# A transformer layer over 1,024 sequences: the order of ScalarE's transfers, and of the turn, cast and split of x, is changed

## The reference, cut to what matters

```
q = x @ wq + bq;  k = x @ wk + bk;  v = x @ wv + bv      # 8 heads of 16
out  = softmax(q k^T / 4) v                               # per head, over 128 tokens
x1   = layernorm(x + out @ wo + bo, ln1_g, ln1_b)
ff   = relu(x1 @ w1 + b1) @ w2 + b2                        # 512 hidden features
y    = layernorm(x1 + ff, ln2_g, ln2_b)
```

## Time and profile before

| | |
|---|---|
| median of three runs | 4492.08 us |
| the profiled execution | 4491.22 us, its span 4489.4 us |
| TensorE busy, matmul and weight load | 4162.2 us (93%), 3558.9 us (79%) |
| VectorE busy | 3687.2 us (82%) |
| ScalarE busy | 3503.9 us (78%) |
| GpSimd busy | 3694.0 us (82%) |
| granted TensorE clock, mean | 0.993 |

### The profile page before, as it was taken

How to read it: one execution, slowest core, us unless ns; L and a number is a source line. 1 busy time by engine, 2 the same in 40 slices (tenths; PEclk the granted TensorE clock), 3 DMA queues, 4 the chain that set the end, 5 groups by cost and what they waited for, 6 DMA issues and landing times.

```text
span 4489.4 us, 150530 instructions
## 1 busy us (share of the span) xinstructions
PE 4162.2 (93%) x49930; PEld 3558.9 (79%) x49930; DVE 3687.2 (82%) x9740; ACT 3503.9 (78%) x5890; POOL 3694.0 (82%) x3864
## 2 busy tenths in 40 slices
PE   5999999999999999999999999999999999999997
PEld 4888787878888888888778788878888887888886
DVE  5888888888888888888888888888888888888885
ACT  3787777778777878777778777878777877778786
POOL 4888888888888888888878888888888888888887
PEclk7999999999999999999999999999999999999999
DMA  7777777777777777777777777777777777777773
GB/s 141 169 168 176 166 176 168 174 167 178 172 170 173 171 173 168 175 169 175 169 170 168 171 169 173 169 173 169 175 167 176 168 176 168 174 169 175 172 171 85
DMA packets 1970442, 755.81 MB, mean 168 GB/s; under 512 B 1181312, under 2 KB 1969536, under 8 KB 1969664
## 3 DMA queue, kind: packets, MB, share of 16 engines
q1 hardware_dynamic: 1662480, 605.71, 60.9%
q10 hardware_dynamic: 307184, 140.40, 11.3%
HBM read 202.51 MB, written 134.22 MB: 75 GB/s over the span
## 4 chain that ended last, share of the span: by engine, by line
PE 23%; POOL 23%; issue 19%; ACT 12%; ACTq 11%; DVE 11%; POOLq 0%; SPq 0%; DMA 0%; DVEq 0%
POOL rs L314 9%; ACTq L459 7%; POOL xT_parts L330 7%; ACT parts L385 6%; PE bankA L740 6%; PE bankA L663 5%; DVE st L557 5%; PE bankC L663 4%; DVE z_sb L581 4%; POOL o_sb L286 3%; ACTq L472 3%; PE sT_ps L714 3%; PE s_ps L700 3%; ACT h_sb L392 2%; ACT v_ones L467 2%
## 5 line engine op out<-in xcount | busy, mean ns | idle before, releaser
L412 ACT ACTIVATE prob_sb<-sT_ps 128x1024 f32<-128x1024 f32 x1024 | 1044.2, 1020 | 238.0 <-PE sT_ps L714 127.5
L540 DVE TENSOR_REDUCE max_sb<-s_ps 128x8 f32<-128x1024 f32 x1024 | 1220.7, 1192 | 8.3 <-PE s_ps L700 7.3
L700 PEld LDWEIGHTS s_ps<-stack 96*128 96x128 bf16 x8192 | 464.5, 98 | 261.8 <-issue 236.6
L700 PE MATMUL s_ps<-stack 96*128 96x128 bf16 x8192 | 640.3, 221 | 17.9 <-DVE max_sb L540 10.3
L714 PE MATMUL sT_ps<-stack 99*128 99x128 bf16 x8192 | 628.6, 219 | 2.3 <-ACT prob_sb L412 2.2
L278 POOL TENSOR_TENSOR parts<-rest_sb,parts 128x512 bf16<-128x512 f32 x512 | 583.7, 1159 | 40.5 <-ACT parts L385 32.9
L392 ACT ACTIVATE h_sb<-bankC,b_col 128x512 f32<-128x512 f32 x512 | 352.0, 688 | 319.1 <-issue 315.5
L434 ACT ACTIVATE n_sb<-z_sb,shift,rs 128x128 f32<-128x128 f32 x1024 | 422.3, 483 | 196.9 <-POOL shift L316 196.9
L727 PE MATMUL oT_ps<-prob_sb,v_ones 128*32 128x128 f32 x16384 | 554.3, 276 | 4.3 <-ACT prob_sb L412 3.3
L686 PE MATMUL bankB<-w_sb,h_sb 128*128 128x128 f32 x4096 | 526.7, 282 | 6.1 <-ACT h_sb L392 5.8
L727 PEld LDWEIGHTS oT_ps<-prob_sb,v_ones 128*32 128x32 f32 x16384 | 416.6, 109 | 127.8 <-issue 90.7
(11 more groups left out here) (75 smaller groups left out, 8919.6 us busy)
## 6 DMA issues: line engine op xcount, KB each, us to landing
stack<-parts SPq DMA_DIRECT2D x3072, 128.0 KB, 3.5
x_blocks<-in_x SPq DMA_DIRECT2D x1024, 64.0 KB, 2.3
n_mem<-n_sb SPq DMA_DIRECT2D x256, 256.0 KB, 2.5
n_blocks<-n_mem SPq DMA_DIRECT2D x1024, 64.0 KB, 2.2
out<-out_sb ACTq DMA_DIRECT2D x256, 256.0 KB, 4.3
x_sb<-in_x ACTq DMA_DIRECT2D x255, 256.0 KB, 3.6
stack<-max_parts ACTq DMA_DIRECT2D x768, 8.0 KB, 2.3
h_sb<-in_L_conv_w SPq DMA_DIRECT2D x1, 256.0 KB, 3.2
```

The costliest lines, as they stand in the source:

```text
L412: act.activation(prob_sb[:, s % 2], sT_ps[:], ACT.Exp, scale=float(D) ** -0.5).then_inc(exp_done, 1)
L540: dve.reduce_max(max_sb[:, (r - lag) % 2, :, s], s_ps[:].rearrange("p (h k) -> p h k", h=H), AX.X).then_inc(max_done, 1)
L700: ins = pe.matmul(s_ps[:, h * P:(h + 1) * P], stack[0:PROD, (r - lag) % 4, 0, h, tok], stack[0:PROD, (r - lag) % 4, 1, h, tok], start=True ...
```

## The change

Four things are written in another order; nothing is added and nothing removed.

1. The three transfers of maxima no longer follow one another: the first stands behind relu 0, the second behind relu 1, the third behind the copy of v.
2. The load of x for the residual moves from the end of step r - 1 to step r, behind the cast of xT.
3. VectorE turns x right after row maximum 0, ahead of z; it was after row maximum 1.
4. ScalarE casts xT right after exponential 0, ahead of relu 2 and 3; it was after the four `n_sb`. GpSimd splits xT ahead of the deviations; it was after the first `normalise`.

```diff
@@ GpSimd
+                if live(t, r, 0):
+                    pool.wait_ge(xT_hi, upto(t, r, 0, plus=1))
+                    if (v := upto(t, r, 0)) is not None:
+                        pool.wait_ge(k_done, v)
+                    pool.tensor_tensor(xT_parts[:, REST], xT_sb[:], xT_parts[:, HI].bitcast(F32),
+                                       ALU.subtract).then_inc(xT_lo, 1)
                 if live(t, r, 5) or live(t, r, 8):
...
                 if live(t, r, 4):
                     normalise(t, r, 0)
-                if live(t, r, 0):
-                    pool.wait_ge(xT_hi, upto(t, r, 0, plus=1))
...
@@ ScalarE
+            def max_row(t, r, part):
+                act.dma_start(stack[PROD + part:PROD + part + 1, (r - 2) % 4, 0],
+                              max_parts[:, part]).then_inc(max_rows_loaded, DMA)
...
                 exponentials(t, r, 0)
+                if live(t, r, 0):
+                    act.wait_ge(x_turned, upto(t, r, 0, plus=1))
+                    if (v := upto(t, r, 0)) is not None:
+                        act.wait_ge(k_done, v)
+                    act.activation(xT_parts[:, HI], xT_sb[:], ACT.Copy).then_inc(xT_hi, 1)
+                if live(t, r, 0) and (r > 0 or not isinstance(t, int)):
+                    if (v := upto(t, r, 1)) is not None:
+                        act.wait_ge(xb_done, v)
+                    act.dma_start(x_sb[:, r % 2], x_g[t + r]).then_inc(x_loaded[r % 2], DMA)
                 if live(t, r, 7):
                     relu(t, r, 7, 2)
                     relu(t, r, 7, 3)
...
                     relu(t, r, 6, 0)
                 if live(t, r, 2):
                     act.wait_ge(max_parts_made, upto(t, r, 2, plus=1))
-                    for part in range(MAXROWS):
-                        act.dma_start(stack[PROD + part:PROD + part + 1, (r - 2) % 4, 0],
-                                      max_parts[:, part]).then_inc(max_rows_loaded, DMA)
+                    max_row(t, r, HI)
                 if live(t, r, 6):
                     relu(t, r, 6, 1)
+                if live(t, r, 2):
+                    max_row(t, r, MID)
...
-                if live(t, r, -1):
-                    if (v := upto(t, r, 0)) is not None:
-                        act.wait_ge(xb_done, v)
-                    act.dma_start(x_sb[:, (r + 1) % 2], x_g[t + (r + 1)]).then_inc(x_loaded[(r + 1) % 2], DMA)
+                if live(t, r, 2):
+                    max_row(t, r, LO)
@@ VectorE
                 row_max(t, r, 0)
+                if live(t, r, 0) and (r > 0 or not isinstance(t, int)):
+                    turn_x(t, r)
                 if live(t, r, 5):
                     dve.wait_ge(wo_done, upto(t, r, 5, plus=1))
...
                 row_max(t, r, 1)
-                if live(t, r, 0) and (r > 0 or not isinstance(t, int)):
-                    turn_x(t, r)
```

More of the change, by code:

```diff
@@ L324, in step @@
                     normalise(t, r, 0)
-                if live(t, r, 0):
-                    pool.wait_ge(xT_hi, upto(t, r, 0, plus=1))
-                    if (v := upto(t, r, 0)) is not None:
-                        pool.wait_ge(k_done, v)
-                    pool.tensor_tensor(xT_parts[:, REST], xT_sb[:], xT_parts[:, HI].bitcast(F32),
-                                       ALU.subtract).then_inc(xT_lo, 1)
                 if live(t, r, 1):
@@ L436, in step @@
                     ins.then_inc(n_done, 1)
[L437 to L441, removed]
                 if live(t, r, 8):
```

## The result

The changed kernel takes 4264.75 us in the median of four runs (4259.5 to 4273.66), the kernel before 4493.6 us in the runs beside it. The ratio is 0.949, 95% interval 0.9469 to 0.9511: 5.1% faster. The direction was right.

The account below looks back on a forecast made before the run. The prediction saw TensorE held by waits for the copy of v and the split; a new loop through turn, cast and relus of 16.42 us plus 0.22 of unknown terms gave 16.64 a step, 4356 us, range 4296 to 4440.

Parts of the forecast that it names:

- Each wait that was named: TensorE's waits for copy of v and split vanish, GpSimd's ahead of the deviations shrinks, 0.3 to 0.7 us appears ahead of `down`.
- The loop that was named: q, exponential 2, rest of q, row maximum 0, turn, cast, relu 2 and 3, `down`, next q: 16.42 us a clean step.
- The load of x: Term between cast and relu 2: bounds 0 and 0.8 us a step, 0.10 taken.
- The two other unknown terms: ScalarE's other long issues, 0.07 us a step taken, and the landing of SyncE's stack, 0.05 taken.
- Its lower end: Lower end of the 8-in-10 range, 4296 us; with no unknown term showing, a 16.42 us step gives 4299 us, chance 0.12.
- rival B: Load of x takes 1.25 to 1.5 us nearly every step, delaying relu 2 and 3: about 4535 us; chance 0.09 with other slowdowns.
- The landing of the stack: Term for scores waiting on SyncE's 12 transfers: bounds 0 and 0.4 us a step, 0.05 taken.
- The other issues: Term for other issues now and then 0.8 us longer: bounds 0 and 0.23 us a step, 0.07 taken.
- Rival A: Issues and stack put the unknown terms near mid-bounds: step 17.0 us, 4415 to 4450 us; chance 0.22.
- The sum by that rule, 4330: Load of x already issued under exponential 0, so its term is nothing: 16.54 us a step, about 4330 us.

Follow-up runs that it names:

- run 256: Not a label of a run: the words say that the kernel's loop is run 256 times, its number of steps.
- the last kernel: Changed kernel with stack issued by parts, turn ahead of row maximum 0, output store behind next step's exponential 1, load of x behind `n_sb`: 4167.56 us, ratio 0.927.
- the edit that takes them away: Changed kernel with SyncE issuing the stack's 12 transfers by part (high, middle, low) instead of waiting for the low parts first: 4253.85 us, ratio 0.9447.

## Why the prediction was wrong in size

**What held.** Each wait that was named went where it was said to go: relu 1 behind relu 0, `wo` free, q free, GpSimd's wait filled, a new wait ahead of `down`, the cast idle 0.35 us for the turn (0.6 was said). The sizes were smaller than said: the wait ahead of `down` 0.24 us in the clean step, where 0.54 stood in the sum, and q 934.53 - 925.21 = 9.32 us after `wo`, where 9.5 to 9.6 stood. The loop that was named is the one that binds in the changed kernel: 0.16 us more from cast to relu 2 lengthen the clean step by 0.14 to 0.15, 0.10 less shorten it by 0.12, the same added work at a place where ScalarE stood idle costs nothing, and with the loop opened by the turn the clean step falls to 15.88.

**The step that failed: the sum of that loop, 16.42 us.** The same pieces in the rows after, with Q = 934.53. The load of x, which the prediction added to this sum as a term of 0.10, stands inside the loop (between the cast and relu 2), so it belongs to the fourth piece:

| piece | predicted | measured |
|---|---|---|
| q to rest of q | 1.95 | 936.39 - 934.53 = 1.86 |
| rest of q to the end of row maximum 0 | 6.09 | 942.40 - 936.39 = 6.01 |
| that end to the end of the turn | 0.60 | 943.01 - 942.40 = 0.61 |
| end of the turn to `down`, with the load | 2.06 + 0.10 | 928.87 - 926.87 = 2.00 |
| `down` to q | 5.72 | 934.53 - 928.87 = 5.66 |
| sum | 16.42 + 0.10 | 16.14 |

Four of five pieces were too long, by 0.06 to 0.16 us, and none was too short by more than 0.01. They are not peculiar to this step: over the shorter half of the steps between 500 and 2500 us the medians are the same within 0.01. Where I chained operations of different lists I put each start behind the end of the one before and a gap; in the trace the high part of q starts 0.11 us ahead of the end of exponential 2. For q behind the turned scores I took 0.48 us, read elsewhere in TensorE's rows; it is 934.53 - 934.11 = 0.42 here. The rows of before had a distance that needs no chain: from q to the end of row maximum 0 they give 940.62 - 932.73 = 7.89 us, where the chain gave 8.04; measured after are 942.40 - 934.53 = 7.87.

On a loop that is run 256 times the sum's error is 0.38 x 256 = 97 us, more than the 91 us that the prediction missed. The two other unknown terms go the other way: 0.07 + 0.05 was taken, and the spans give (4489.4 - 4271.9) / 256 = 0.85 us less than 17.17, so 16.32 and an excess of 0.18 over the clean step; that takes some 15 us off the miss. It is 10 us wider again since the profiled execution, at 4273.66, is the slowest of four after the change.

**The range failed by the same step.** Its lower end was the clean sum with all unknown terms at zero, as if the sum itself could only be too short. The rows allowed more: by the prediction's own pieces TensorE alone needs 15.88, and bounds of 15.88 to 16.42 for the loop would have put the lower end at about 4160. That floor was itself too high: the last kernel's clean step is 15.76.

**The terms.** The load of x: taken 0.10, measured 0.12 in the clean step (16.14 to 16.02 without it); its long cases, the whole of rival B, did not occur once in the 255 of the whole span, whose longest is 0.434 us. The landing of the stack: taken 0.05; the waits are 24 to 41 us over the span, 0.09 to 0.16 a step, but the edit that takes them away gave back 0.04 to 0.08. The other issues: taken 0.07; the 11 long steps that show such an issue and no wait for the stack hold 6.9 us beyond the clean step in 122 steps, 0.06 a step, and shorter delays come on top. Rival A's mechanism is thus there, though not its price.

**What the prediction didn't ask.** It never priced the first part by itself. Its own pieces give 6.86 + 9.33 = 16.19, less than the 16.42 that it forecast for both parts together. Had that stood in the text, either the second part would have been called a loss or the 16.42 been doubted. Both pieces of the 16.19 are long distances in TensorE's own rows, and that sum came out right: 16.16 was measured. The measured 16.16 and 16.14 say: the second part exchanges one loop for another of the same length. With the further edits, which open the new loop, the kernel gets to 15.76; whether edits to the old loop would have done as much with the first part alone wasn't tried.

The rule of the Trainium skill (page "Perfetto Trace Analysis", section "Sequencer Loop") that an engine's instruction waits in a queue while the sequencer goes on did not show here as the prediction applied it, with the load issued under exponential 0: the load of x starts 0.18 us after the end of the turn (926.87 to 927.05), so it was held as long as the cast ahead of it waited. The load's own wait can't be what held it, since it had been met over 8 us earlier. The sum by that rule, 4330, would have been nearer to the result, but for a wrong reason.

## What to carry to other kernels

Price each part of a change by its own loop before pricing them together; if a part alone comes out shorter than the whole, either one of the two sums is wrong or the other part is a loss. A sum over a loop that is chained from ends and gaps came out 0.38 us too long here, spread over four pieces (0.06 to 0.16 us each), while the two sums that rested on long distances read in one go (q to the end of row maximum 0, and the old loop without the transfers) held within 0.03. So read the longest distance that the rows of before have in one go, and give the sum a lower bound too, by the busiest engine's own list. In a loop this balanced the next bound stands 0.1 us behind the one removed: what the load gave was taken back, mostly at the landing of the stack.

## What the runs showed of the hardware that was not expected

A transfer written behind a ScalarE operation is issued when that operation's wait is over, not when it starts. In the hardware loop of the changed kernel the load of x follows the end of the turn by 0.17 us in the median (0.04 in the steps ahead of and behind the loop), also where the cast itself is still queued behind exponential 0: in the long step shown above the load is issued at 1826.16, 0.20 us after the turn's end, and the cast starts at 1826.78 only. So a transfer behind an operation that waits is covered by that operation's length, and by nothing of the wait. The same steps show what an issue costs between two operations: relu 2 starts 0.642 us after the cast in the 182 steps in which the load is issued between them, and 0.518 us in 67 in which it was issued ahead of the cast.

The load of x took 0.401 us in the median and 0.428 at most in 61 issues at its new place, against 0.426 and 1.535 in 58 at the old one, with SyncE issuing its stack at both. What goes with the long ones is the distance to ScalarE's own issue before. Over the twelve traces, each from 190 us on, 1153 of the 10273 issues that began within 0.6 us of the end of the one before took over 0.9 us (11%), 3 of the 266 that began 0.6 to 1 us behind it, and none of the 4280 that began later. The last kernel, one of the twelve, shows it best: with the store and the load each apart from other transfers, none of 511 took more than 0.505 us, where 43 of 256 stores took over 0.9 us in the changed kernel. No run varied this distance alone, so it is a rule of these traces and not a cause that is shown.
